# One more gathered chunk a turn moves from the indirect gathers to row-by-row fetches, shared by SyncE and ScalarE

## The reference

```python
agg = segment_sum(layernorm(x)[src], dst, num_segments=N)     # E = 106250 edges, sorted by dst, 17 a node
h = relu(agg @ W_rel + b_rel + layernorm(x) @ W_root)          # 512 wide
i, f, g, o = split(h @ W_ih.T + b_ih + b_hh); c = sigmoid(i) * tanh(g)
x = x + (sigmoid(o) * tanh(c)) @ W_fc + b_fc
w = softmax(((layernorm(x) @ W_x + b_x) @ W_slice + b_slice) / temperature)   # 8 heads x 64 slices
x = x + attention over the slice tokens, spread back with w, @ W_out + b_out
```

## Time and profile before

| what | value |
|---|---|
| timed runs | 1239.16, 1241.82, 1243.43 us; median 1241.82 us |
| the profiled execution | 1240.34 us, its span 1238.5 us |
| PE busy | 1116.1 us (90%), clock granted 0.994 of full over the span |
| POOL busy | 805.3 us (65%), of which the 798 gathers of L700 763.5 us |
| DVE, ACT busy | 831.8 us (67%), 627.2 us (51%) |
| DMA | 188.74 MB, 152 GB/s; 1920 row fetches by SP |

### The profile page before, as it was taken

The page is one execution under the profiler, slowest core; times in us unless marked ns, Lnnn a source line. Parts: engine busy times, 40 slices in busy tenths (PEclk is TensorE's granted clock), DMA queues, the critical chain, the costliest instruction groups (busy, mean ns, idle before and its releaser), DMA issues. The chain is left out here.

```text
span 1238.5 us, 30254 instructions
## 1 busy us (share of the span) xinstructions
PE 1116.1 (90%) x9821; PEld 967.1 (78%) x9821; DVE 831.8 (67%) x2560; ACT 627.2 (51%) x1257; POOL 805.3 (65%) x856
## 2 busy tenths in 40 slices
PE   1077799999999999999999999999999999999998
PEld 0046688878888888788888787888888878897798
DVE  7885476667666766676677756775767566746665
ACT  5872444554456454545554545455545454555332
POOL 5877777777777777777777777777777777400000
PEclk9998999999999999999999999999999999999999
DMA  8674444444454445444544444444444454313498
GB/s 313 225 268 119 125 130 136 147 142 136 129 148 142 141 124 150 140 140 123 150 149 138 121 148 150 137 121 150 147 136 122 150 149 137 97 44 116 129 336 290
DMA packets 92966, 188.74 MB, mean 152 GB/s; under 512 B 20914, under 2 KB 55591, under 8 KB 92821
## 3 DMA queue, kind: packets, MB, share of 16 engines
q0 software_dynamic: 39168, 107.01, 30.0%
q1 hardware_dynamic: 42794, 59.89, 14.8%
q10 hardware_dynamic: 10859, 20.05, 4.5%
HBM read 154.87 MB, written 32.00 MB: 151 GB/s over the span
## 5 line engine op out<-in xcount | busy, mean ns | idle before, releaser
L700 POOL DMA_INDIRECT ring<-table,sidx x798 | 763.5, 957 | 247.5 <-issue 242.7
L419 PE MATMUL ps<-h_h,wih_h 128*128 128x250 f32 x1200 | 338.8, 282 | 0.0
L420 PE MATMUL ps<-h_l,wih_h 128*128 128x250 f32 x1200 | 336.5, 280 | 0.0
L421 PE MATMUL ps<-h_h,wih_l 128*128 128x250 f32 x1200 | 336.5, 280 | 0.0
L419 PEld LDWEIGHTS ps<-h_h,wih_h 128*128 128x128 f32 x1200 | 230.1, 192 | 2.0 <-issue 0.8
L420 PEld LDWEIGHTS ps<-h_l,wih_h 128*128 128x128 f32 x1200 | 230.2, 192 | 1.1
L421 PEld LDWEIGHTS ps<-h_h,wih_l 128*128 128x128 f32 x1200 | 230.1, 192 | 0.0
L850 ACT ACTIVATE gate<-ps,bgate 128x250 f32<-128x250 f32 x300 | 124.2, 467 | 140.7 <-PE ps L421 139.7
L651 DVE TENSOR_SCALAR oneh<-iota,didx 128x64 f16<-128x64 f16 (+2 forms) x1179 | 183.1, 259 | 0.0
L1078 PE MATMUL ps<-ring,oneh 128*32 128x512 f16 x2280 | 151.0, 391 | 34.5 <-DMA ring<-table,sidx 31.9
L1078 PEld LDWEIGHTS ps<-ring,oneh 128*32 128x32 f16 x2280 | 59.5, 97 | 107.7 <-DMA ring<-table,sidx 46.4
(11 more groups left out here) (213 smaller groups left out, 2508.4 us busy)
## 6 DMA issues: line engine op xcount, KB each, us to landing
sp_ring<-table SPq DMA_DIRECT2D x1920, 1.0 KB
ring<-table,sidx POOLq DMA_INDIRECT x798
swt_d<-swt ACTq DMA_DIRECT2D x25, 500.0 KB
gate<-swt_d SPq DMA_DIRECT2D x19, 500.0 KB, 5.9
x_room<-in_x SPq DMA_DIRECT2D x12, 512.0 KB, 10.6
xn<-table SPq DMA_DIRECT2D x25, 224.0 KB
xin<-in_x SPq DMA_DIRECT2D x25, 224.0 KB
res<-xin SPq DMA_DIRECT2D x25, 224.0 KB
```

What stands on the lines that cost most here:

```text
L419: eng.matmul(dst, wh, xh, start=first, stop=False)
L420: eng.matmul(dst, wh, xl, start=False, stop=False)
L421: return eng.matmul(dst, wl, xh, start=False, stop=last)
L700: pool.indirect_dma_start(ring[:, j, :], None, table, bass.IndirectOffsetOnAxis(ap=idx, axis=0)).then_inc(done, 16)
```

## The change

The chunks that are fetched row by row start at 86 as before, but come every 33 chunks, 23 in place of 15; POOL gathers the other 808. Of the 128 rows of such a chunk SP fetches the first 78, in three register loads of 26, and ACT the other 50, in five register loads of 10. SP's rows behind its other DMAs become 6, 14 and 60 a turn, and 78 at the start. ACT fetches 30 rows before its first turn, 20 behind `split_x` in turn 1, and later up to 49 a turn at the places below. ACT's turns are now written out, since the rows stand at different places of a chunk in each.

```diff
-    SP_FIRST, SP_STEP, SP_N, SP_SLOTS = 86, 52, 15, 3
+    SP_FIRST, SP_STEP, SP_N, SP_SLOTS = 86, 33, 23, 3
-    ROWS_FIRST, ROWS, LOADS = 96, (8, 16, 60), 32
+    ROWS_FIRST, ROWS, LOADS = 78, (6, 14, 60), 26
+    SP_ROWS = 3 * LOADS
+    ACT_ROWS = P - SP_ROWS
+    ACT_FIRST, ACT_LOADS = 30, 10
...
+            def load_rows():
+                r = loaded[0]
+                if r < last_row and r < row_at[0] + 2 * ACT_LOADS:
+                    k, q = r // ACT_ROWS, r % ACT_ROWS
+                    if q == 0:
+                        wait_slot(act, k)
+                    for i, start in enumerate(load_starts(act, k, SP_ROWS + q, ACT_LOADS)):
+                        starts[r + i] = start
+                    loaded[0] += ACT_LOADS
...
             def turn(t, odd, gather, gnn, ffn, ahead):
+                if t == 0:
+                    for _ in range(ACT_FIRST // ACT_LOADS):
+                        load_rows()
+                        fetch_rows(ACT_LOADS)
                 if gnn:
                     split_x(t - 1)
+                    for _ in range(1 if ffn else 2):
+                        load_rows()
+                        fetch_rows(10)
                     relu_h(t - 1, 0)
+                    fetch_rows(1)
...
                     gates(t - 1, 10, 12)
+                    fetch_rows(2)
                     high_hl(t - 1, 0)
                     tanh_c(t - 1, 3)
+                    fetch_rows(1)
...
                     act.dma_start(swt_d[ds(p, 1)].rearrange("a p n -> p (a n)"),
                                   swt[:, :, :, :].rearrange("p e j n -> p (e j n)")).then_inc(swt_st, 16)
+                    load_rows()
+                    fetch_rows(2)
...
-            with act.Fori(lo, hi, step) as t:
+            for t in range(lo, hi, step):
                 two_turns(turn, t)
```

More of the change, by code:

```diff
@@ L438, in out_count, with wait_slot, load_starts, fetch_row @@
             return 16 * (len(range(q, NCH + 1, TILES)) + (len(REST_PARTS) - 1 if q == NCH % TILES else 0))
+        rows8 = table.bitcast(U8).rearrange("n c -> (n c)")
+        row_bytes = 4 * C
+        def wait_slot(eng, k):
+            if k == 0:
+                eng.wait_ge(spi_done, 1)
+            if k >= SP_SLOTS:
+                b = last_reader(SP_CHUNKS[k - SP_SLOTS])
+                eng.wait_ge(sum_done[b % 2], b // 2 + 1)
+                eng.wait_ge(sum_done[(b - 1) % 2], (b - 1) // 2 + 1)
+        def load_starts(eng, k, q, n):
+            _, at = nc.values_load_multi_w_load_instructions(
+                sp_idx[k:k + 1, q:q + n], engines=[eng.engine], min_val=0, max_val=(N - 1) * row_bytes,
+                skip_runtime_bounds_check_because="the DMA checks its bounds")
+            return at
+        def fetch_row(eng, k, q, start):
+            to = sp_ring[q:q + 1, k % SP_SLOTS, :].bitcast(U8)
+            eng.dma_start(to, rows8[ds(start, row_bytes)].rearrange("(p c) -> p c", p=1)).then_inc(
+                sp_rows[k % SP_SLOTS], 16)
         @block.sync
@@ L517, in _ @@
             row_at = [0]
-            rows8 = table.bitcast(U8).rearrange("n c -> (n c)")
-            row_bytes = 4 * C
             def fetch_rows(n):
-                for r in range(row_at[0], min(row_at[0] + n, SP_N * P)):
-                    k, q = r // P, r % P
+                for r in range(row_at[0], min(row_at[0] + n, SP_N * SP_ROWS)):
+                    k, q = r // SP_ROWS, r % SP_ROWS
                     if q == 0:
[L526 to L531, removed]
-                    if q % LOADS == 0:
[L533 to L539, removed]
+                        wait_slot(sp, k)
+                    if q % LOADS == 0:
+                        starts[:] = load_starts(sp, k, q, LOADS)
+                    fetch_row(sp, k, q, starts[q % LOADS])
                 row_at[0] += n
@@ L548, in turn @@
                     for j, k in SP_OF.items():
-                        assert first_reader(j) // 2 > t or row_at[0] >= (k + 1) * P, (t, j, k, row_at)
+                        assert first_reader(j) // 2 > t or row_at[0] >= (k + 1) * SP_ROWS, (t, j, k, row_at)
                 if gather:
@@ L579, in _ @@
             last_turns(turn)
-            assert row_at[0] >= SP_N * P
+            assert row_at[0] >= SP_N * SP_ROWS
             def f_load(n, k):
@@ L873, in copy_out, with fetch_rows @@
                                ACT.Copy).then_inc(att_a, 1)
-            def turn(t, odd, gather, gnn, ffn, ahead):
+            row_at, loaded, starts = [0], [0], {}
+            last_row = SP_N * ACT_ROWS
+            def load_rows():
[7 more added lines that the diff above has]
+                    loaded[0] += ACT_LOADS
+            def fetch_rows(n):
+                for r in range(row_at[0], min(row_at[0] + n, loaded[0])):
+                    fetch_row(act, r // ACT_ROWS, SP_ROWS + r % ACT_ROWS, starts.pop(r))
+                    row_at[0] += 1
+            def turn(t, odd, gather, gnn, ffn, ahead):
+                if gather and t < NP - 1:
+                    for j, k in SP_OF.items():
+                        assert first_reader(j) // 2 > t or row_at[0] >= (k + 1) * ACT_ROWS, (t, j, k, row_at)
+                if t == 0:
+                    for _ in range(ACT_FIRST // ACT_LOADS):
+                        load_rows()
+                        fetch_rows(ACT_LOADS)
                 if gnn:
                     split_x(t - 1)
+                    for _ in range(1 if ffn else 2):
+                        load_rows()
+                        fetch_rows(10)
                     relu_h(t - 1, 0)
+                    fetch_rows(1)
                 if ffn:
@@ L890, in turn @@
                 if gnn:
-                    gates(t - 1, 0, 4)
+                    fetch_rows(3)
+                    gates(t - 1, 0, 2)
+                    load_rows()
+                    fetch_rows(2)
+                    gates(t - 1, 2, 4)
                     tanh_c(t - 1, 0)
+                    load_rows()
+                    fetch_rows(8)
                 if ffn:
@@ L901, in turn @@
                 if gnn:
-                    gates(t - 1, 4, 8)
+                    gates(t - 1, 4, 6)
+                    fetch_rows(1)
+                    gates(t - 1, 6, 8)
+                    fetch_rows(1)
                     tanh_c(t - 1, 1)
+                    fetch_rows(3)
                     gates(t - 1, 8, 10)
+                    load_rows()
+                    fetch_rows(3)
                 if ffn:
@@ L936, in _ @@
             lo, hi, step = turns(turn)
-            with act.Fori(lo, hi, step) as t:
+            for t in range(lo, hi, step):
                 two_turns(turn, t)
             last_turns(turn)
+            assert row_at[0] == last_row
             def f_high(n, k):
```

## The result

The changed kernel took 1276.38 us (median; 1274.45 to 1279.45) against 1242.32 us for the kernel before on the same chip: ratio 1.0282, 95% interval 1.0257 to 1.0307. It is 34 us slower; 1232.0 was forecast, with 1248 as the upper end. The profiled execution has a span of 1272.6 us at a granted clock of 0.99.

The account below looks back on a forecast made before the run. POOL's gathers, at 41.0 us a turn, were taken as the bound. 1240.3 - 10.1 (eight gathers fewer) + 1.0 (two close paces) = 1231.2 us against the profiled execution; forecast 1232.0, range 1227.5 to 1248.

Parts of the forecast that it names:

- Two paces: Main turns: POOL's gathers go at 41.0 us a turn, PE with ACT and DVE at 39.96; the slower counts.
- A row on ACT: ACT's sequencer: a 1 KB row fetch costs 0.32 us as on SP, with ends 0.29 and 0.41.
- SP's waits: SP, late in a turn: waiting up to some 6 us for that turn's odd sums costs nothing.
- A load of 10: ACT's register load of ten addresses: 0.96 us, on a line between 0.486 (one register) and 2.134 (32).
- The place behind the store: ACT, a load and two rows before `split_x`: its end moves from 513.27 to 514.1, costing nothing by itself.
- The place before `relu_h`: ACT, a load and ten rows in its 4.30 us wait: wait used up, 0 to 0.4 us a turn, 0.2 taken.
- Two rows behind the last gates: ACT, before `hl_h`: two rows of 0.64 us delay it and PE's output layer, 0.3 us a turn.
- The sum of 0.5 us for rows: ACT's tight places together lengthen PE's path by 0.5 us a turn, under the 0.58 at which PE becomes slower.
- The start: Before the first turns: ACT's rows and loads make PE's cell begin at 117.5, 4.5 us late, at cost 0.
- The sign named for a wrong forecast: PE's waits for gathered rows gone and turns over 40.5 us: ACT is slower, forecast wrong by 2.2 us per 0.1.
- The dear loads: Rival on ACT: a load of 10 costs what one of 32 does, 2.8 us a turn, 1279 us; chance 0.05.
- Dear rows: Rival on ACT: a row takes 0.41 us of its sequencer, 1.8 us a turn, 1257 us; chance 0.17.

Follow-up runs that it names:

- the run with one load: Changed kernel with one register load on ACT in place of 115, its ten addresses serving all rows ACT fetches: 1230.62 us, ratio 0.9898.
- the run with 84 rows a turn: Changed kernel, SP fetching 84 rows a turn in loads of 20, ACT loads of 12, from multiples of four, none behind `swt` store: 1238.28 us, ratio 0.9991.
- The probe: Kernel before, with 43 register loads behind the end of SP's program and 8 behind ACT's, each followed by one row fetch: one execution, 1336.63 us.

## Why the prediction was wrong, point by point

- **Two paces, POOL at 41.0, PE at 39.96:** right. Without loads POOL is again the bound, its gathers (1056.7 - 60.3) / 789 = 1.263 us apart, its last start at 1056.7, where 1058 was forecast.
- **A row on ACT, 0.32 us:** right; ten behind a load take 3.44 us, eight in the run with one load 2.58. **SP's waits, nothing:** right here; the run with 84 rows a turn shows that they can cost.
- **A load of 10, 0.96 us on a straight line: the step that failed.** It is 1.17 us from a multiple of four words, 2.37 from elsewhere, and about 1 us more behind the store. The load of 32, on which the line rests, had been measured only at multiples of four. SP's load of 26, put at 1.81, was 2.05 to 2.15 and 5.6; that cost nothing, as the run with one load on ACT shows.
- **The place behind the store, "nothing by itself":** fell with the load: `split_x` came 3.24 us later behind the store, not 0.8, and PE stood 0.4 to 1.9 us a turn. **The place before `relu_h`, 0.2:** right in kind, at most 0.3 us while an even start stood there, 1.2 to 1.5 where an odd one did.
- **Two rows behind the last gates, 0.3 us a turn:** wrong, 0. The sum of 0.5 us for rows was too high.
- **The start:** the cell at 118.14, forecast 117.5. POOL stood 3.53 us at 141.36, forecast none: of the 5.3 us in hand 2.0 were gone, since POOL began that much earlier, and the sums came 5.9 us late, with a cell forecast 4.5 late.
- **The sign named for a wrong forecast** worked: PE's waits for rows gone, a turn of 42.63, (42.63 - 40.54) x 22 = 46 us over 1231, that is 1277.
- **Rivals.** The dear loads, 1279, were given 0.05 and came within 3 us, though not because a load of 10 costs what one of 32 does: it costs half of that or, from an odd start, a little more. An unknown price between 0.49 and 2.13 us, twice in line against a margin of 0.58 us a turn, decides the sign; its upper end deserved a far greater chance, and the range should have reached it. Dear rows and a dear loop: no.

The Trainium skill, "Runtime: NRT & Kernel Launch", section "Instruction fetch mechanics", gives about 200 ns a register. The prediction set that aside for the load of 32. The probe shows both: 0.20 us a register from word 2, 0.22 for four from word 0. The prediction's estimate of 1276 us by that figure is near the measured time by luck: away from the store ACT's loads took 1.17 or 2.37 us, not 2.0. On the scale of the prediction's 1279 the sum is 1240.3 + 879.1 + 22 x (0.5 + 2 x 1.04) - 902.0 = 1274.

## What to carry to other kernels

A price read from a trace holds for the sizes and the addresses that the trace has: ask in what the new use differs besides its size. Where one unknown price stands in line several times and its bounds straddle the margin, measure it, or forecast both outcomes with real weight. And a helper queue that may run ahead must be paced to what is used, since its next wait has other work behind it.

## What the runs showed of the hardware

- A register load from SBUF took about 0.3 us and 0.20 to 0.22 us an access. From a start at a multiple of four words (16 bytes) of its row that fits four words an access, with left-over words singly; from any other start it fits one word an access, also past the next such multiple (32 words from word 2: 6.74 us; from word 0: 2.10).
- A load of 10 behind the issue of the 500 KB store took 1.9 to 2.3 us in place of 1.17, and loads of 26 on SP that began at about the same time 2.5 to 3.3 in place of 2.05.
- A 1 KB row fetch by ACT took 0.32 us of its sequencer, as on SP; up to 49 a turn cost nothing that shows (ratio 0.9898, with one load on ACT).
